# Layer 0's first transfers of a two-layer decoder, divided between the sync queue and ScalarE's queue

## What is computed

```python
def _L0_attn_ref(x, Wq, Wk, Wv, Wo):
    q, k, v = (proj(Wq), proj(Wk), proj(Wv))          # 16 heads of 16
    att = jnp.einsum('bhqd,bhkd->bhqk', q, k) / jnp.sqrt(jnp.float32(D))
    att = jax.nn.softmax(jnp.where(causal, att, -jnp.inf), axis=-1)
    out = jnp.einsum('bhqk,bhkd->bhqd', att, v)
    return out.transpose(0, 2, 1, 3).reshape(Bsz, Tlen, C) @ Wo.T

x = _layernorm(x + _L0_attn_ref(...))
x = _layernorm(x + _L0_xattn_ref(x, ctx_2048, ...))    # theta, phi, g, softmax, norm, relu, out_w
x = _layernorm(x + _L0_ffn_ref(...))                   # 4-bit weights with scales, plus low-rank factors
x = _layernorm(x + _L1_attn_ref(...))                  # 16 heads of 128
x = _layernorm(x + _L1_xattn_ref(x, ctx_2048, ctx_2048))
x = _layernorm(x + _L1_ffn_ref(...))                   # 64 experts, top 8
```

## Time and profile before

| what | value |
|---|---|
| median of 3 runs | 806.86 us (805.07 to 808.9) |
| span of the profiled execution | 803.3 us |
| the profiled execution's own total | not given on the page; what lies around the span comes on top |
| PE busy | 726.7 us (90% of the span) |
| DVE, ACT, POOL busy | 513.3, 331.8, 308.4 us |
| traffic | HBM read 102.36 MB, written 35.58 MB |

### The profile page before, as it was taken

One profiled execution on the slowest core, in us unless ns is written; L12 is line 12 of the kernel. 1 busy time (PEld: TensorE's weight loads), 2 busy tenths in 40 slices (PEclk: granted clock), 3 DMA queues, 4 the chain that ended last, 5 costly groups with the idle time before them and its releaser, 6 DMA issues.

```text
span 803.3 us, 16549 instructions
## 1 busy us (share of the span) xinstructions
PE 726.7 (90%) x5482; PEld 594.9 (74%) x5482; DVE 513.3 (64%) x1681; ACT 331.8 (41%) x874; POOL 308.4 (38%) x400
## 2 busy tenths in 40 slices
PE   6999999999899999999998688750899999999997
PEld 4677777776788888888886355430789999999966
DVE  4788787775466666666668778730556666655526
ACT  4454556442343343434342355530334444444433
POOL 1112121322115121212112037777256666666656
PEclk9899999999999999999999999975899999999999
DMA  9344080000024242335323247932479999955456
GB/s 235 89 126 125 15 282 15 7 1 1 20 90 128 74 145 74 128 106 138 87 67 115 48 133 226 329 104 111 125 235 283 303 290 308 368 169 164 130 220 264
DMA packets 80375, 118.03 MB, mean 147 GB/s; under 512 B 27927, under 2 KB 57213, under 8 KB 79012
## 3 DMA queue, kind: packets, MB, share of 16 engines
q1 hardware_dynamic: 69972, 98.58, 39.9%
q0 software_dynamic: 9168, 17.35, 6.0%
q10 hardware_dynamic: 1152, 1.05, 0.4%
HBM read 102.36 MB, written 35.58 MB: 172 GB/s over the span
## 4 chain that ended last, share of the span: by engine, by line
PE 73%; POOL 10%; DMA 5%; issue 5%; DVE 4%; ACT 2%; SPq 2%; DVEq 0%; POOLq 0%; ACTq 0%
PE ps L171 66%; POOL x_slots L1633 8%; PE ps L174 7%; DMA rowso<-y_slots 3%; DVE topc L1536 1%; DMA x<-in_x_in 1%; DMA rows_e<-x_slots 1%; ACT pTc L1481 1%; SPq L318 1%; POOL y_slots L1994 1%; POOL mvc L188 0%; SPq L2038 0%; DMA x_slots<-rows_all,index_all 0%; ACT eT L539 0%; DMA y_slots<-o_e,index_e 0%
## 5 line engine op out<-in xcount | busy, mean ns | idle before, releaser
L1994 POOL DMA_INDIRECT y_slots<-o_e,index_e x127 | 124.3, 979 | 85.2 <-issue 59.4
L171 PE MATMUL ps<-xT_e,w_slot 128*128 128x128 f32 x760 | 100.4, 275 | 0.0
L171 PEld LDWEIGHTS ps<-xT_e,w_slot 128*128 128x128 f32 x760 | 92.4, 192 | 0.1
L1973 DVE TENSOR_TENSOR h_e<-ps,gate_e 128x128 f32<-128x128 f32 x127 | 37.0, 292 | 76.9 <-ACT gate_e L1936 76.3
L1930 ACT COPY xT_e<-ps 128x256 f32<-128x256 f32 x127 | 47.3, 372 | 69.6 <-PE ps L174 69.4
L1633 POOL DMA_INDIRECT x_slots<-rows_all,index_all x64 | 62.7, 980 | 19.7 <-issue 18.1
L174 PE MATMUL ps<-ident,rows_e 128*128 128x128 f32 x254 | 49.5, 277 | 21.3 <-DMA rows_e<-x_slots 21.3
L171 PE MATMUL ps<-x_hi,w_hi 128*128 128x512 f32 x192 | 62.9, 409 | 2.6 <-DVE x_lo L1043 1.5
L1936 ACT ACTIVATE gate_e<-ps 128x128 f32<-128x128 f32 x127 | 35.3, 278 | 67.9 <-PE ps L171 67.4
L174 PEld LDWEIGHTS ps<-ident,rows_e 128*128 128x128 f32 x254 | 35.6, 143 | 34.1 <-DMA rows_e<-x_slots 22.1
L171 PE MATMUL ps<-x_lo,w_hi 128*128 128x512 f32 x192 | 60.1, 394 | 0.0
(11 more groups left out here) (296 smaller groups left out, 1725.0 us busy)
## 6 DMA issues: line engine op xcount, KB each, us to landing
w_slot<-in_we SPq DMA_DIRECT2D x95, 384.0 KB
rows_e<-x_slots SPq DMA_DIRECT2D x127, 136.0 KB
x_slots<-blank SPq DMA_DIRECT2D x4, 2176.0 KB, 10.1
rowso<-y_slots SPq DMA_DIRECT2D x8, 1024.0 KB, 11.8
sums<-key_sums SPq DMA_DIRECT2D x15, 512.0 KB, 4.5
w_kept<-in_we SPq DMA_DIRECT2D x20, 384.0 KB, 4.8
wh<-in_wqkv SPq DMA_DIRECT2D x16, 384.0 KB, 5.5
w_early<-in_we SPq DMA_DIRECT2D x12, 384.0 KB, 5.2
```

Source lines behind the costliest of these rows:

```text
L171: return self.pe.matmul(out, lhsT, rhs, start=start, stop=stop, skip_group_check=shared)
L1973: dve.tensor_tensor(T.h[:, :], T.g_bank[:, P:2 * P], T.gate[:, :], ALU.mult).then_inc(*t.h.one)
L1994: pool.indirect_dma_start(m.y_slots, bass.IndirectOffsetOnAxis(ap=T.index[:, :], axis=0), T.o[:, :], None, bounds_check=TOK * TOPK - 1, oo ...
```

## The change

Sixteen transfers go from the sync engine to ACT. ACT issues x of sequences 0 and 1 as its first instructions, ahead of its table load. After its copy of the turned x of sequence 0, and ahead of `kpair`, it issues the four low-rank factors, ctx of sequences 0 and 1 and the eight tables. The sync engine keeps the attention weights, the quantised weights and the scales, and then goes on as before with x of sequence 2. Semaphores and their counts are the same.

```diff
-    sp.dma_start(t.lanes[0].x[:, :], a["x_in"][0, :, :]).then_inc(*t.x_in[0].one)
     sp.dma_start(t.w0[:, 0:2, :, :], a["w0"][:, 0:2, :, :]).then_inc(*t.wqk_in.one)
     sp.dma_start(t.w0[:, 2:4, :, :], a["w0"][:, 2:4, :, :]).then_inc(*t.wvo_in.one)
-    for dst, src in ((t.upa, a["upa"]), (t.upb, a["upb"]), (t.dna, a["dna"]), (t.dnb, a["dnb"])):
-        sp.dma_start(dst[:, :], src).then_inc(*t.lora_in.one)
     quantised(t.up_in, t.upq, a["upq"], t.ups, a["ups"])
-    sp.dma_start(t.lanes[0].ctx[:, :], a["ctx_in"][0, :, :]).then_inc(*t.ctx_in[0].one)
-    for dst, src in ((t.th[:, :, :], a["thw"]), (t.outw[:, :], a["outw"]), (t.b64[:, :], a["bias64"]),
-                     (t.b128[:, :], a["bias128"]), (t.gb[:, :], a["gb"].broadcast_to([P, LAT])), (t.gamma[:, :], a["gamma"]),
-                     (t.beta[:, :], a["beta"]), (t.bdn[:, :], a["bdn"].broadcast_to([P, D]))):
-        sp.dma_start(dst, src).then_inc(*t.table_in.one)
-    load_x(1)
-    load_ctx(1)
     quantised(t.dn_in, t.dnq, a["dnq"], t.dns, a["dns"])
...
+def act_first_x(m, a, t):
+
+    for b in range(LANES):
+        m.act.dma_start(t.lanes[b].x[:, :], a["x_in"][b, :, :]).then_inc(*t.x_in[b].one)
+
+
+def act_tables(m, a, t):
+
+    act = m.act
+    for dst, src in ((t.upa, a["upa"]), (t.upb, a["upb"]), (t.dna, a["dna"]), (t.dnb, a["dnb"])):
+        act.dma_start(dst[:, :], src).then_inc(*t.lora_in.one)
+    for b in range(LANES):
+        act.dma_start(t.lanes[b].ctx[:, :], a["ctx_in"][b, :, :]).then_inc(*t.ctx_in[b].one)
+    for dst, src in ((t.th[:, :, :], a["thw"]), (t.outw[:, :], a["outw"]), (t.b64[:, :], a["bias64"]),
+                     (t.b128[:, :], a["bias128"]), (t.gb[:, :], a["gb"].broadcast_to([P, LAT])), (t.gamma[:, :], a["gamma"]),
+                     (t.beta[:, :], a["beta"]), (t.bdn[:, :], a["bdn"].broadcast_to([P, D]))):
+        act.dma_start(dst, src).then_inc(*t.table_in.one)
...
-def act_layer0(m, t, t1):
+def act_layer0(m, a, t, t1):
     act = m.act
+    act_first_x(m, a, t)
     act.preload_act_table(ACT.Exp)
     act.wait_ge(*t.identb_set(1))
...
         act.wait_ge(*t.xT_ps(b + 1))
         act.copy(t.xT[:, :, :].rearrange("p k t -> p (k t)"), b2[:, 0:D]).then_inc(*t.xT_set.one)
+        if b == 0:
+            act_tables(m, a, t)
         yield
```

More of the change, by code:

```diff
@@ L2160, in program_pe, with program_act @@
     pe_combine(m, s.to, s.te)
-def program_act(m, s, out):
-    act_layer0(m, s.t0, s.t1)
+def program_act(m, a, s, out):
+    act_layer0(m, a, s.t0, s.t1)
     after_layer0(m.act, s.t0)
@@ L2227, in decoder @@
         program_pe(m, s)
-        program_act(m, s, out)
+        program_act(m, a, s, out)
         program_dve(m, s)
```

## The result

The changed kernel takes 811.79 us (median of 19 runs, 810.01 to 815.63) against 807.16 us (19 runs, 802.9 to 810.61) of the kernel before. The ratio is 1.0063, with a 95% interval of 1.0045 to 1.008: slower by 4.6 us in the medians. The forecast was 810.7 us, no change at its upper edge, with 0.38 for slower by over 0.5%. The time lies in the range, but on the other side of the edge: slower by a little over 0.5%. The profiled execution took 814.11 us with a span of 812.7, so 1.4 us lie around a span.

A forecast was written before the change was run, and what follows sets the result against it. PE (73% of the chain) was taken to bound the kernel, with layer 0's start carried to the end. +3.05 (ACT's issues) +1.7 (clock) -0.9 (x of sequence 1) = +3.85 us on 806.86: 810.7 us, range 805.7 to 814.

The forecast's parts named there:

- ACT's 14 issues: Between ACT's xT copy and `kpair`: 14 issues take 7.52 us, `kpair` at 12.9, scores at 14.0, +3.05 us.
- the low bound of 0.43 an issue: Same 14 issues at ACT's own end-of-kernel price: 6.0 us, `q` ends at 12.5, the term is +1.5 us.
- x of sequence 0: First load, now sharing DMA engines with the Q and K weights: taken as hidden, 0, bounds 0 to +0.6 us.
- ctx and the tables: First needed behind the sums of the scores; on their way by 13, so they stay hidden.
- The split of the scores' delay: Start of sequence 0's scores: late x(0) taken as 0, ACT's 14 issues as +3.05 us.
- The clock: PE's longer gap before the scores leaves them at half clock, 3.84 us instead of 2.12: +1.7, bounds 0 to +2.6.
- x of sequence 1, -0.9: Issued near 1.3 instead of 11.13, PE's 0.98 us wait can go; output products start sooner, -0.9 us at most.
- The sum at the output products: Terms +3.05, +1.7 and -0.9 give +3.85 us, carried from layer 0's start to the end.
- The rivals: Clock stays up or issues cheaper (0.24); ACT's issues held up by sync's (0.20); issues hidden in ACT's idle time (0.10).
- Hidden issues: Rival: 14 issues take 2.1 us inside ACT's 4.17 us idle time before `kpair`; total 805.7 us, chance 0.10.

The follow-up runs named there:

- x(0) on sync: Changed kernel with x of sequence 0 back on sync as its first transfer, the 14 issues staying on ACT; ratio to the kernel before 1.0082.
- only x on ACT: Changed kernel with the 14 other transfers back on sync, so ACT issues only x of sequences 0 and 1; ratio to the kernel before 1.0011.
- early matmuls: Kernel before plus 7 unread matmuls on PE ahead of the constants and 2 behind the first transposes; ratio to the kernel before 1.0019.
- 14 behind `q`: Changed kernel with ACT's 14 issues moved behind its first `kpair` and `q`, ahead of the exponentials; ratio to the kernel before 1.0076.
- four on ACT: Changed kernel with ACT issuing only x and the four low-rank factors, the ten other transfers back on sync; ratio to the kernel before 1.0014.

## Why the prediction was right, and where it was not

The direction and the main mechanism held. The size of the sum held partly by luck, as several terms were off in opposite directions. Point by point:

- **ACT's 14 issues.** Priced at 7.52 us, measured 7.3; `kpair` forecast at 12.9, measured 13.48; the scores at 14.0, measured 14.72. Pricing them by sync's rows for the same transfers was right, and the low bound of 0.43 an issue was not.
- **x of sequence 0.** Taken as hidden, with a bound of +0.6. It landed 4.42 us after its issue instead of 2.1, and `xT` is 1.12 us later. This is the term that was put at nothing and wasn't, and the source of the 0.6 at `kpair`: a small transfer that used to go ahead of the weights now runs among them. The Trainium skill (DMA: Bandwidth & Descriptors, Queues, rings and completion order) says that each DMA engine takes turns between queues, packet by packet; the rows agree so far as x holds PE until 5.26 to 5.62 in every kernel in which it is on its own queue beside the weights, and lands within 3.0 us in the one with x(0) back on sync, ahead of them. But the kernel with x(0) back on sync shows that little is to be won by mending it alone: `kpair` comes 0.24 us sooner.
- **ctx and the tables.** Taken as hidden. In the changed kernel they were: DVE's sums let POOL go. With x(0) on sync they weren't, and PE waited 1.21 us.
- **The split of the scores' delay.** Of +3.73 us, 1.53 are there with only x on ACT (late x and V at half clock), and 2.20 come with the 14 issues. I had it as 0 and +3.05. The split depends on the order in which the causes are taken: with x(0) on sync and the 14 issues in place the scores are still 3.50 us late.
- **The clock.** Forecast +1.7 in the scores. From the first score to the first top it takes 2.59 us in the first profile, 3.41 in the second, 3.90 in the kernel with x(0) on sync, against 2.13 before: +0.5, +1.3 and +1.8. The forecast's 3.84 for scores wholly at half clock is the third of these. The clock fell at 16.2, 15.4 and 12.0 in them, so the size is a matter of when in an execution it falls. The same fall also stretched the low-rank products to 3.62 us, which I had as a bound only. That the early Q and K products ran at half clock is borne out by the early matmuls.
- **x of sequence 1, -0.9.** Its wait is gone, and the delay does shrink, from 5.57 us at the first transpose to 4.11 at the output products. But the early issue needn't have done this: PE's wait for x(1) ended at 20.23 and 21.45 in the two profiles of before, and PE comes to it at 24.33 now, when even the old order would have had it there. And x(1) alone, moved early on sync, brought no measurable time.
- **The sum at the output products.** Forecast 20.85 + 3.85 = 24.7; measured 24.96 and 25.90. In the first profile the parts are: scores +3.73 (forecast 3.05), from there to the first top +0.46 (1.7), from the top to the first transpose +1.38 (0), from there to the output products -1.46 (-0.9). The errors, +0.68, -1.24, +1.38 and -0.56, nearly cancel: that the sum came out to 0.3 us is luck, not precision. In total +3.85 forecast, +4.6 measured (19 runs each).
- **The rivals.** In the changed kernel sync is done at 5.64, before ACT begins at 6.13, so sync's issues can't hold up ACT's. Longer issues exist (x(0) on sync), and their cause isn't shown. Hidden issues: those of up to four are hidden, 14 are not.

## What to carry to other kernels

A transfer moved to a compute engine's queue costs that engine's time at the place where it is issued, here 0.52 us each (7.3 us for 14): add up the issues, compare them with the idle stretch they go into, and move no more than fits (four did, eleven and fourteen didn't). What the issuing engine does next becomes late; a transfer can too, if it is issued so late that someone waits for it (4.52 us with the 14 issues behind `q`). And where single executions differ by a clock that falls at other places, size a change of half a per cent by early rows that are stable and by many runs, not by two spans.

## What was not expected of the hardware

- The record of the granted clock begins with 1.00, but the first products of PE take 3.79 us where the same ones take 2.36 behind 4.7 us of other matmuls (early matmuls). The record is not to be believed at the start; durations of equal instructions are.
- ACT starts an issue 0.02 us after the start of the copy ahead of it (6.11 and 6.13), so an issue runs beside the instructions ahead of it in the program. With 14 behind `q` the first two issues (10.69, 11.06) run beside both halves of `kpair` and `q` (10.68, 11.06, 11.41), which keep their usual times. It is only what stands behind the issues that waits.
- The same issues aren't always equally long: ACT's two of ctx took 1.35 us with x(0) on sync and 0.93 in the changed kernel, with sync issuing at the time in neither. Issues on both queues at once kept their usual lengths (four on ACT).
- In the kernel before, the wait for x of sequence 1 ended at 20.23 in one execution and at 21.45 in another, though everything that PE did before was within 0.2 us. The last table was what POOL waited for in the second one only.
